# Twelve expert blocks of the first ten token tiles, worked from a table of their own while the last tiles are routed

## The chip, the cores and the metric

One core of one Trainium2 chip runs the whole program. Its engines are TensorE (PE), VectorE (DVE), ScalarE (ACT), GpSimd (POOL) and SyncE (SP), each with its own list of instructions that it works through in order; they wait for one another on semaphores. SP issues most of the DMA transfers, ACT some, POOL the indirect ones (gathers and scatters through a list of indices). The metric is the device time of one execution in microseconds; lower is better.

## The reference, cut to what matters

The program computes four layers on 2048 tokens (16 tiles of 128) of width 512. The change concerns the border between the first and the second:

```python
x = x + _L0_xattn_ref(_layernorm(x), ctx, seg, ...)      # attention, 16 heads
x = x + _L0_ffn_ref(_layernorm(x), gate_w, ...)          # mixture of experts
#   scores = softmax(h @ gate_w.T); topk_w, topk_idx = top_k(scores, 6)
#   for e in range(16):
#       y += cw[:, e] * ((silu(h @ w_gate[e].T) * (h @ w_up[e].T)) @ w_down[e].T)
x = x + _L1_xattn_ref(_layernorm(x), ctx, mask)
x = x + _L1_ffn_ref(_layernorm(x), ...)
```

Every token goes to 6 of 16 experts of inner width 352.

## The kernel before, in words

**Attention.** The loop runs over 64 steps `m` (`STEPS`): tile `m // 4`, four heads each. It is software pipelined: scores of step m, transposes of m-2, values of m-3, output products of m-4. Beside it run three side jobs: splitting the expert weights into two float16 halves in DRAM (`split_load`, `split_act`, `split_dve`, `split_store`, 128 pieces), writing the finished tiles' normalized rows to `token_rows` in DRAM (`row_stats`, `row_rstd`, `row_normalize`, `row_high`, `row_low`, `row_store`), and routing. Routing a tile is: transpose its rows (`token_rows` on PE), `logits`, softmax, the best six (`route_best`), a mask, `ranks` (a running count per expert by matmul), `route_rank`, and six indirect DMAs of POOL (`place`) that write each token's number to its place in the list of its expert (`recs`, `expert_tokens` in the trace). The last attention steps and the routing of tiles 14 and 15 stand behind the loop as code written out by hand.

**The table.** After tile 15, PE sums the counts of all experts (`count`), DVE makes a table of 111 blocks from it (L2007 to L2030), PE turns its columns into one row (`cols`), and DVE copies the row to `tabrow`. A block is up to 128 tokens of one expert; the row holds for each block the tile of `recs` where its list stands, the expert, and the slot of its weights.

**Experts.** SP waits for the table, for all stores and for all placements, then loads the lists (`records`, one DMA of 128 numbers a block), and the weights into a ring of 4 slots: `first_a` and `first_d` for the first four experts, `expert_loads` and `down_loads` for later ones (issued for each block and executed only at the last block of an expert). POOL gathers the token rows of a block (`gather_rows`, ring of 6). PE turns them (`turn_rows`), makes gate and up products (`expert_up`), turns the hidden values (`turn_hidden`) and makes the down product (`expert_down`); ACT scales it (`rows_out`, ring of 3), and POOL adds it to `x_sum` in DRAM by an indirect DMA that must have landed before the next is issued. The first blocks of every engine are a hand-written order of these calls.

What sets the order everywhere is the program text: no scheduler moves anything.

## Time and profile before

| | us |
|---|---|
| median of 3 runs | 1945.56 (1942.91 to 1946.44) |
| the profiled execution | 1929.01 |
| its span | 1927.2 |
| PE busy | 1803.6 (94%) |
| DVE busy | 1096.7 (57%) |
| ACT busy | 886.3 (46%) |
| POOL busy | 819.4 (43%) |

The profiled execution is 16.55 us shorter than the median of the runs. The span is what the trace covers; 1.8 us lie around it. A row of `windows` gives for a stretch of the span the busy time of each engine, the granted clock of PE as a share of full speed (1.00 is 2.4 GHz, 0.50 is 1.2 GHz), the share of time in which the DMA engines were busy, and what they moved. A row of a timeline gives the start, the duration, the engine, the line, the operation and, in brackets, how long the engine had been idle and what released it.

### The profile page before, as it was taken

How to read it: one execution, taken by the hardware profiler on the slowest of the kernel's cores; microseconds unless marked ns; L12 is line 12 of the kernel's file. 1: busy time of each engine (PE TensorE's matmuls, PEld its weight loads, DVE VectorE, ACT ScalarE, POOL GpSimd, SP SyncE). 2: the span in 40 equal slices, each digit the busy share in tenths (PEclk: the TensorE clock that was granted, in tenths of full speed). 3: DMA queues.
4: the chain of work that ended last, by engine and by line, in shares of the span. 5: the costliest groups of instructions: out<-in, count | busy, mean ns of one | idle time of the engine just before them, and what ended most of it. 6: DMA issues, size and time to landing. Idle time of an engine off the chain costs nothing.

```text
span 1927.2 us, 39654 instructions
## 1 busy us (share of the span) xinstructions
PE 1803.6 (94%) x12786; PEld 1075.3 (56%) x12789; DVE 1096.7 (57%) x2985; ACT 886.3 (46%) x1833; POOL 819.4 (43%) x731
## 2 busy tenths in 40 slices
PE   6989999999982999999999999995899999999998
PEld 3566667666641666666666666664644444444444
DVE  4678887888862333322323223223756877777776
ACT  4578878878851443434434434443832121122211
POOL 4224456666564334444443443442112434554442
PEclk8999999999986999999999999997999999999999
DMA  8255598878886566666666665545012355555653
GB/s 309 88 153 175 177 140 182 188 166 175 184 183 181 143 147 141 155 165 149 153 155 142 155 152 100 90 85 129 33 35 72 124 182 201 205 170 209 208 174 144
DMA packets 156354, 294.83 MB, mean 153 GB/s; under 512 B 41248, under 2 KB 91040, under 8 KB 152032
## 3 DMA queue, kind: packets, MB, share of 16 engines
q1 hardware_dynamic: 105184, 157.48, 30.4%
q0 software_dynamic: 46368, 126.29, 26.8%
q10 hardware_dynamic: 4608, 8.52, 1.6%
q8 instruction: 115, 1.88, 0.4%
q14 instruction: 79, 0.65, 0.1%
HBM read 426.00 MB, written 78.33 MB: 262 GB/s over the span
## 4 chain that ended last, share of the span: by engine, by line
PE 63%; DMA 15%; DVE 9%; issue 6%; ACT 5%; SPq 1%; POOL 1%; POOLq 0%; ACTq 0%; DVEq 0%
PE bank L235 16%; PE bank L236 16%; PE bank L237 16%; DMA x_sum<-x,work_arena 10%; DVE work_arena L1580 2%; PE bank L1064 2%; ACT xt_arena L1316 2%; DMA work_arena<-in_moe_w 2%; PE bank L854 1%; PE bank L1091 1%; DVE xt_arena L1580 1%; PE bank L1175 1%; DMA expert_w<-xt_arena 1%; DMA x<-token_rows,work_arena 1%; DVE xt_arena L1663 1%
## 5 line engine op out<-in xcount | busy, mean ns | idle before, releaser
L235 PE MATMUL bank<-work_arena,xt_arena 128*128 x1221 | 404.6, 331 | 2.8 <-DVE xt_arena L2074 1.9
L237 PE MATMUL bank<-work_arena,xt_arena 128*128 x1221 | 404.5, 331 | 0.0
L236 PE MATMUL bank<-work_arena,xt_arena 128*128 x1221 | 404.5, 331 | 0.0
L2313 POOL DMA_INDIRECT x_sum<-x,work_arena x111 | 175.9, 1585 | 397.7 <-DMA x_sum<-x,work_arena 197.2
L2062 DVE TENSOR_TENSOR xt_arena<-xt_arena,bank 128x352 f32<-128x352 f32 x111 | 57.9, 522 | 406.2 <-PE bank L237 406.2
L235 PE MATMUL bank<-work_arena 128*128 128x512 f16 (+1 forms) x600 | 226.8, 379 | 13.9 <-DVE x L1885 6.7
L236 PE MATMUL bank<-work_arena 128*128 128x512 f16 (+1 forms) x600 | 226.7, 379 | 0.0
L237 PE MATMUL bank<-work_arena 128*128 128x512 f16 (+1 forms) x600 | 226.6, 379 | 0.0
L1470 ACT ACTIVATE xt_arena<-bank 128x1024 f16<-128x1024 f16 x111 | 113.6, 1023 | 224.8 <-PE bank L1064 224.8
L235 PE MATMUL bank<-xt_arena,work_arena 128*128 128x512 f16 x528 | 200.4, 380 | 1.8 <-DVE xt_arena L195 1.8
L236 PE MATMUL bank<-xt_arena,work_arena 128*128 128x512 f16 x528 | 200.3, 379 | 0.0
L237 PE MATMUL bank<-xt_arena,work_arena 128*128 128x512 f16 x528 | 200.1, 379 | 0.0
L2320 POOL TENSOR_TENSOR work_arena<-work_arena 128x512 f16<-128x512 f32 x64 | 73.2, 1163 | 269.1 <-ACT work_arena L1455 269.1
L237 PEld LDWEIGHTS bank<-work_arena,xt_arena 128*128 128x128 f16 x1221 | 119.7, 98 | 85.0
L235 PEld LDWEIGHTS bank<-work_arena,xt_arena 128*128 128x128 f16 x1221 | 119.7, 98 | 82.6 <-issue 3.3
L236 PEld LDWEIGHTS bank<-work_arena,xt_arena 128*128 128x128 f16 x1221 | 119.7, 98 | 79.4
L2329 POOL DMA_INDIRECT work_arena<-in_pk_e,work_arena x128 | 135.0, 1055 | 36.8 <-issue 34.1
L1580 DVE SCALAR_TENSOR_TENSOR work_arena<-work_arena 128x704 f16<-128x704 f32 (+2 forms) x90 | 89.6, 997 | 73.3 <-ACT work_arena L1363 72.6
L2300 POOL DMA_INDIRECT x<-token_rows,work_arena x111 | 110.8, 999 | 46.3 <-issue 28.7
L2214 POOL TENSOR_TENSOR xt_arena<-xt_arena,work_arena 128x512 f32<-128x512 f32 x64 | 66.9, 1045 | 143.7 <-DVE work_arena L1670 137.7
L1316 ACT ACTIVATE xt_arena<-xt_arena,work_arena 128x128 f32<-128x128 f32 x256 | 123.2, 482 | 2.1
L1885 DVE SCALAR_TENSOR_TENSOR x<-bank,x 128x512 f32<-128x512 f32 x128 | 88.2, 691 | 60.4 <-PE bank L237 60.4
(278 smaller groups left out, 3817.5 us busy)
## 6 DMA issues: line engine op xcount, KB each, us to landing
work_arena<-expert_w SPq DMA_DIRECT2D x111, 1408.0 KB
work_arena<-expert_w SPq DMA_DIRECT2D x111, 768.0 KB
work_arena<-in_moe_w SPq DMA_DIRECT2D x64, 352.0 KB
expert_w<-work_arena SPq DMA_DIRECT2D x128, 176.0 KB
work_arena<-in_moe_w SPq DMA_DIRECT2D x64, 192.0 KB
expert_w<-xt_arena SPq DMA_DIRECT2D x128, 96.0 KB
work_arena<-in_mlp_w SPq DMA_DIRECT2D x8, 1536.0 KB, 9.0
work_arena<-in_head_w SPq DMA_DIRECT2D x16, 512.0 KB, 5.2
```

Source lines behind the costliest of these rows:

```text
L235: pe.matmul(o, a_hi, b_hi, start=start, stop=False)
L236: pe.matmul(o, a_hi, b_lo, start=False, stop=False)
L237: return pe.matmul(o, a_lo, b_hi, start=False, stop=stop)
L1316: last = act.activation(prob[:, m % 3, i, :], prob[:, m % 3, i, :], ACT.Exp, bias=ebias[:, m % 4, i:i + 1], scale=seg_scale[:, t:t + 1], a ...
L1470: act.activation(xT[:, b % 2, :], bank[4][:, :].bitcast(F16), ACT.Copy).then_inc(xt_cp, 1)
L1580: return dve.scalar_tensor_tensor(out=o, in0=src, scalar=scale, in1=hi, op0=ALU.mult, op1=ALU.subtract)
L1885: dve.scalar_tensor_tensor(out=xv, in0=bank[6 + q % 2][:, :], scalar=1 / (WS * WS), in1=xv, op0=ALU.mult, op1=ALU.add).then_inc(xadd[q % 2 ...
L2214: pool.tensor_tensor(prob[:, m % 3, :, :], prob[:, m % 3, :, :], rinv[:, m % 4, :].unsqueeze(2).to_broadcast([P, 4, P]), ALU.mult).then_in ...
L2300: pool.indirect_dma_start(out=xbu[:, b % XB, :], out_offset=None, in_=rows[:, :], in_offset=bass.IndirectOffsetOnAxis(ap=rid[:, i:i + 1], ...
L2313: pool.indirect_dma_start(out=xacc[:, :], out_offset=bass.IndirectOffsetOnAxis(ap=rid[:, i:i + 1], axis=0), in_=ysb[:, b % YB, :], in_offs ...
L2320: pool.tensor_tensor(h_lo[:, S_ % 2, c, :], m2[:, c, :], h_hi[:, S_ % 2, c, :], ALU.subtract).then_inc(hlo, 1)
L2329: pool.indirect_dma_start(out=gbuf[:, n % 2 * SETS + i - FIRST[n], :], out_offset=None, in_=ins["pk_e"][:, :], in_offset=bass.IndirectOffs ...
```

## The change

The list places of the first ten tiles are known well before the last tiles are routed. The new kernel counts the experts after tile 9 (`early_count`), makes a first table of the 12 first whole blocks in expert order (`early_blocks`, `early_columns`, `early_row`), and starts the expert stage with them. The tokens of tiles 0 to 9 give each expert 10 x 128 x 6 / 16 = 480 on average, which is three whole blocks, so that the twelve belong to about four experts; these are loaded again for the rest of their tokens. The last attention output, the rows of tile 15, its logits, mask, ranks and placements, the full count, the second table (`main_blocks`, `main_columns`, `main_row`) and its lists are moved in between the first expert blocks. The number of blocks is 111 as before. In outline (the diff, cut):

```diff
+EARLY_TILES, EARLY = 10, 12
+EARLY_Y = 9
@@ SP
             for e in range(E):
+                if e == E - 1:
+                    sp.wait_ge(yadd, 1)
+                    sp.dma_start(xacc[T:T + P, :], x[:, 0, :]).then_inc(xacc_early, 16)
+                    sp.wait_ge(rope_h, 2 * NT)
+                    sp.wait_ge(rope_l, 2 * NT)
+                    sp.dma_start(rc2, ins["route_c2"]).then_inc(route_in, 16)
                 for i in range(e * NPC, (e + 1) * NPC):
                     split_store(i)
...
-            sp.wait_ge(routed, TABLE_ROW)
+            sp.wait_ge(q_free, q_at["early_cols",] + 1)
...
+            sp.wait_ge(placed_early, 16 * TOPE * EARLY_TILES)
             records(0)
+            for s in range(STAGES):
+                sp.wait_ge(split_out[s], 32 * len(range(s, E * NPC, STAGES)))
+            sp.wait_ge(q_mm, q_at["heads", NT - 1, 3] + 1)
+            firsts = [first_expert(r) for r in range(SLOTS)]
+            first_a(0, firsts[0])
+            for r in range(SLOTS - 1):
+                first_d(r, firsts[r])
             records(1)
+            records(2)
+            sp.wait_ge(y_mm, STEPS)
+            first_a(1, firsts[1])
+            first_a(2, firsts[2])
+            first_d(3, firsts[3])
+            first_a(3, firsts[3])
             for b in range(NBLK + 5):
+                if b == EARLY_Y:
+                    sp.wait_ge(routed, TABLE_ROW)
...
+                    sp.wait_ge(placed, 16 * TOPE * (NT - EARLY_TILES))
+                    records(3)
+                    records(4)
@@ PE
-            pe.wait_ge(routed, TABLE_ROW)
+            pe.wait_ge(q_free, q_at["early_cols",] + 1)
             slots = {b: slot_of(b) for b in range(2)}
             turn_rows(0)
+            outputs(STEPS - 1)
+            expert_up(0, slots[0])
             turn_rows(1)
-            expert_up(0, slots[0])
             for b in range(NBLK - 3):
                 expert_up(b + 1, slots[b + 1])
+                if b == 0:
+                    token_rows(15)
+                if b == 1:
+                    logits(15)
+                if b + 2 == EARLY:
+                    pe.wait_ge(routed, TABLE_ROW)
                 slots[b + 2] = slot_of(b + 2)
                 turn_rows(b + 2)
                 turn_hidden(b)
                 if b > 0:
                     expert_down(b - 1, slots.pop(b - 1))
+                if b == 2:
+                    ranks(Q15)
+                if b == 3:
+                    route_count()
+                if b == 5:
+                    route_cols()
@@ DVE
+                if m == STEPS - 3:
+                    early_blocks()
+                if m == STEPS - 2:
+                    early_columns()
                 split_dve(m, 0)
...
             split_dve(STEPS - 1, 1)
+            early_row()
             add_outputs(14)
...
+                if b == 1:
+                    keep_logits(15)
+                    route_scores(Q15)
+                    route_softmax(Q15)
+                    route_best(Q15)
+                    route_mask(Q15)
+                if b == 2:
+                    route_rank(Q15)
+                if b == 3:
+                    main_blocks()
+                    main_columns()
+                if b == 5:
+                    main_row()
@@ POOL
+            normalize(STEPS - 1)
+            gather_rows(0)
+            gather_rows(1)
+            row_rstd(14)
+            row_low(14)
+            gather_rows(2)
+            gather_rows(3)
+            place_batch(INNER - 1, 0, TOPE)
+            gather_rows(4)
+            gather_rows(5)
+            place_batch(Q14, 0, 1)
+            row_rstd(15)
+            row_low(15)
+            place_batch(Q14, 1, TOPE)
+            gather_rows(6)
             for b in range(NBLK):
-                if b + ROWS_AHEAD < NBLK:
+                if b == 1:
+                    place_batch(Q15, 0, TOPE)
+                if ROWS_AHEAD + 2 <= b + ROWS_AHEAD < NBLK:
                     gather_rows(b + ROWS_AHEAD)
                 pool.wait_ge(y_cp, b + 1)
```

The first nine blocks put their down product into one PSUM bank (`y_bank`, bank 6) instead of two, since bank 7 holds the routing of tile 15 (logits, ranks, count, columns). On ACT, `row_high(15)`, `rows_turned(15)`, `gate_exps(Q15)` and `row_store(15)` move between the first blocks, and some small buffers move to other places in SBUF.

POOL, from the normalization of attention step 63 on. Lines of before: L2214 is that normalization, L2220 and L2224 are `row_rstd` and `row_low`, L2228 a placement, L2300 a gather, L2313 the addition to `x_sum`.

```order
L2214 TENSOR_TENSOR xt_arena<-xt_arena,work_arena 128x512 [waits recip]
L2220 TENSOR_TENSOR ln_rs<-ln_ve,neg_half 128x1 [waits t_stat]
L2224 TENSOR_TENSOR xt_arena<-xt_arena 128x512 [waits row_hi]
L2228 DMA expert_tokens<-work_arena 38784x1 [waits indexed]
L2228 DMA expert_tokens<-work_arena 38784x1 x5
L2228 DMA expert_tokens<-work_arena 38784x1 [waits indexed]
L2220 TENSOR_TENSOR ln_rs<-ln_ve,neg_half 128x1 [waits t_stat]
L2224 TENSOR_TENSOR xt_arena<-xt_arena 128x512 [waits row_hi]
```

Now, with the same operations at L2404, L2410, L2414, L2418, L2476 and L2504:

```order
L2404 TENSOR_TENSOR xt_arena<-xt_arena,work_arena 128x512 [waits recip]
L2476 DMA x<-token_rows,xt_arena 128x528 [waits rec_in0]
L2476 DMA x<-token_rows,xt_arena 128x528
L2410 TENSOR_TENSOR ln_rs<-ln_ve,neg_half 128x1 [waits t_stat]
L2414 TENSOR_TENSOR xt_arena<-xt_arena 128x512 [waits row_hi]
L2476 DMA x<-token_rows,xt_arena 128x528 x2
L2418 DMA expert_tokens<-work_arena 38784x1 [waits indexed]
L2418 DMA expert_tokens<-work_arena 38784x1 x5
L2476 DMA x<-token_rows,xt_arena 128x528 [waits rec_in1]
```

Two gathers, the first of which waits for the lists of blocks 0 to 3 (`rec_in0`), now stand ahead of the `row_rstd` and `row_low` of tile 14.

PE, behind the last but one attention output. Before, the last output (the second row), then tile 15 (L955, L235), its ranks (L973), the count (L1050), the table's columns (L1054), and only then the first rows of an expert block (L1064). In the fences that follow, the further rows of the same products are left out.

```order
L955 MATMUL bank<-id,xt_arena 128x128 [waits tr_cp,row_lo]
L955 MATMUL bank<-id,xt_arena 128x128 x7
L235 MATMUL bank<-xt_arena 128x16 [waits q_free,gate_s,tr_cp]
...
L973 MATMUL bank<-work_arena,xt_arena 128x16 [waits q_free,masked]
...
L1050 MATMUL bank<-work_arena,xt_arena 128x16 [waits q_free,masked]
L1054 MATMUL bank<-id,work_arena 1x128 [waits q_free,routed]
...
L1064 MATMUL bank<-id,x 128x128 [waits xb_in0]
```

Now the ranks of tile 14 (L1021), the rows of block 0 (L1125), the last attention output (the first L240), and the up products of block 0 (the L240 that waits for `load_a0`):

```order
L1021 MATMUL bank<-work_arena,xt_arena 128x16 [waits q_free,masked]
...
L1129 TENSOR_LOAD xt_arena [waits q_free]
...
L1125 MATMUL bank<-id,x 128x128 [waits smax,xb_in0]
L1125 MATMUL bank<-id,x 128x128 x7
L240 MATMUL bank<-work_arena 128x512 [waits otl]
...
L240 ISA [waits load_a0,e_xt_cp]
```

The chain over tile 15, count and columns is no longer ahead of the first block.

## Rows read from the trace of the kernel before

**Rows 1.** Windows: length; busy us of PE, PEld, DVE, ACT, POOL; clock, DMA share, GB/s.

```profile
620.00:625.00 5.00, 5.00 (x31) 3.13 (x30) 1.30 (x4) 1.18 (x3) 0.00 (x0) 0.89 1.02 422
667.00:717.00 50.00, 50.00 (x375) 31.79 (x374) 14.88 (x40) 20.14 (x32) 18.27 (x15) 1.00 0.69 167
```

**Rows 2.** Waits of PE between 550 and 660 us: total, times, longest.

```profile
PE bank L1064 <- DMA x<-token_rows,work_arena: 19.9, 1, 19.9
```

**Rows 3.** Chain that ended last, 525 to 620 us: start, us, what.

```profile
548.88 11.35 DMA work_arena<-in_moe_w
596.70 8.67 DMA expert_tokens<-work_arena
```

**Rows 4.** Timeline of PE.

```profile
568.17 0.62 PE L955 MATMUL bank<-id,xt_arena 128*128 128x128 f16 x8
577.75 0.38 PE L237 MATMUL bank<-work_arena 128*128 128x512 f16 x1
614.36 1.04 PE L1064 MATMUL bank<-id,x 128*128 128x128 f16 x8 [19.94 <-DMA x<-token_rows,work_arena]
617.40 0.50 PE L235 MATMUL bank<-work_arena,xt_arena 128*128 x1
621.14 0.31 PE L236 MATMUL bank<-work_arena,xt_arena 128*128 x1
```

**Rows 5.** Timeline of DVE.

```profile
550.42 0.89 DVE L1580 SCALAR_TENSOR_TENSOR work_arena<-work_arena 128x704 f16<-128x704 f32 x1 [2.68 <-ACT work_arena L1363]
560.81 0.56 DVE L1580 SCALAR_TENSOR_TENSOR xt_arena<-work_arena,xt_arena 128x384 f16<-128x384 f32 x1 [0.57 <-ACT xt_arena L1363]
589.82 0.41 DVE L2007 TENSOR_TENSOR work_arena<-bank,work_arena 128x240 f32<-128x240 f32 x1 [0.30 <-PE bank L1050]
591.25 0.17 DVE L2014 TENSOR_SCALAR work_arena<-work_arena 128x16 f32<-128x16 f32 x1
593.73 0.15 DVE L2030 SCALAR_TENSOR_TENSOR work_arena<-work_arena 128x1 f16<-128x1 f32 x1
```

**Rows 6.** Timeline of POOL.

```profile
562.14 1.03 POOL L2214 TENSOR_TENSOR xt_arena<-xt_arena,work_arena 128x512 f32<-128x512 f32 x1 [0.58 <-DVE work_arena L1670]
563.18 0.57 POOL L2220 TENSOR_TENSOR ln_rs<-ln_ve,neg_half 128x1 f32<-128x1 f32 x1
566.96 1.16 POOL L2224 TENSOR_TENSOR xt_arena<-xt_arena 128x512 f16<-128x512 f32 x1 [3.21 <-ACT xt_arena L1335]
594.14 0.97 POOL L2228 DMA_INDIRECT expert_tokens<-work_arena  x1 [0.30 <-issue]
609.26 2.64 POOL L2300 DMA_INDIRECT x<-token_rows,work_arena  x1 [11.60 <-DMA work_arena<-expert_tokens]
612.21 1.05 POOL L2300 DMA_INDIRECT x<-token_rows,work_arena  x1 [0.30 <-issue]
```

**Rows 7.** Timeline of SP's queue.

```profile
605.44 0.34 SPq L768 DMA_DIRECT2D work_arena<-expert_tokens  x1
606.84 7.38 SPq L717 DMA_DIRECT2D work_arena<-expert_tokens  x7
614.27 0.43 SPq L695 DMA_DIRECT2D work_arena<-expert_w  x1
```

**Rows 8.** Transfers to `x_sum`, 600 to 760 us: landing; two of them on POOL.

```profile
DMA to landing us min/median/max: 4.6/4.9/10.3
682.78 1.58 POOL L2313 DMA_INDIRECT x_sum<-x,work_arena  x1 [2.85 <-DMA x_sum<-x,work_arena]
688.31 1.58 POOL L2313 DMA_INDIRECT x_sum<-x,work_arena  x1 [2.65 <-DMA x_sum<-x,work_arena]
```

**Rows 9.** Gathers, 600 to 624 us: landing; then two turns of a block on PE.

```profile
DMA to landing us min/median/max: 7.3/7.6/7.9
675.89 0.61 PE L1064 MATMUL bank<-id,x 128*128 128x128 f16 x8
682.20 0.61 PE L1064 MATMUL bank<-id,x 128*128 128x128 f16 x8
```

More of the change, by code:

```diff
@@ L397, in build @@
         Q14, Q15 = INNER, INNER + 1
+        EARLY_Q = next(q for q, (a, _) in enumerate(BATCHES) if a == EARLY_TILES)
+        COUNT_AT = ready(EARLY_Q) + 2
         def batch_of(t):
@@ L1027, in _ @@
                     outputs(m - 4)
+                if m == COUNT_AT:
+                    pe.wait_ge(masked, EARLY_Q + 1)
+                    q_room_free(pe, "early_count")
+                    pe.matmul(q_bank("early_count")[:, 0:E], one16, seen16, start=True, stop=True).then_inc(q_mm, 1)
                 if m in RANK_AT:
                     ranks(RANK_AT[m])
+            pe.wait_ge(routed, EARLY_SET)
+            q_room_free(pe, "early_cols")
+            for i in range(4):
+                last = pe.matmul(q_bank("early_cols")[0:1, i * P:(i + 1) * P], tcol16[:, i:i + 1], id16[:, :],
+                                 start=True, stop=True)
+            last.then_inc(q_mm, 1)
             turn_prob(STEPS - 2)
@@ L2040, in memory_masks, with main_row @@
+            def main_row():
+                dve.wait_ge(q_mm, q_at["cols",] + 1)
+                n = NBLK - EARLY
+                for i in range(3):
+                    m = dve.tensor_copy(tabrow[0:1, i * P + EARLY:i * P + NBLK],
+                                        q_bank("cols")[0:1, i * P:i * P + n])
+                m.then_inc(routed, 1)
             def memory_masks(part):
@@ L2077, in _ @@
                 dve.memset(t[:, :, MOE_D:], 0.0)
+            add_outputs(15)
+            row_stats(15)
+            for s in range(STAGES):
+                dve.wait_ge(split_out[s], 32 * len(range(s, E * NPC, STAGES)))
+            choose(0, EARLY, early_end)
+            row_normalize(15)
+            expert_weight(0)
             hidden(0)
```

348 lines of the change are left out of this document (210 added, 138 removed).

## The prediction

> **What bounds the kernel now.** I read the windows over the span first, then the waits of PE around the border of attention and experts, then the chain that ended last, then the timelines of PE, DVE, POOL and SP there. Over the expert stage PE is the bound: 50.00 of 50 us busy between 667 and 717, DVE 14.88, ACT 20.14, POOL 18.27 [rows 1], one block each 6.31 us (675.89 to 682.20) [rows 9]. That stage holds the same 111 blocks afterwards and has nothing to give. What can be given is the border. The last attention output ends at 578.1, the first up product of an expert starts at 617.40: 39.3 us with only the short products of tile 15 in them [rows 4]. Its longest part is one wait of 19.94 us for the gathered rows [rows 2, 4]. The chain tells why: POOL's last placement starts at 596.70 and lands 8.67 us later [rows 3], SP fetches the first list at 605.44, POOL can gather at 609.26, PE has the rows at 614.36 [rows 4, 6, 7]. All of it hangs on tile 15, the last to be routed.
>
> **What goes.** The first blocks no longer wait for tile 15, its placements, the count and the table. If nothing else were late, the up product of block 0 would follow the last output at once: 617.40 - 578.1 = 39.3 us. So the question is what is late next. I follow three chains.
>
> **The early table on DVE.** `early_blocks` is 11 instructions, five of them 240 to 256 elements wide. The widest of before took 0.41 us, a small one 0.17, and the 18 instructions of the table of before needed 593.88 - 589.82 = 4.06 us with their waits on each other [rows 5]. 5 x 0.43 + 6 x 0.18 = 3.2 us, and `early_columns`, 30 small ones at 0.17, 5.1 us. They stand in attention steps 61 and 62. The first is ahead of a split of expert weights and of the maxima of step 62, so its 3.2 us pass to ScalarE's exponentials and the next split, and on; it also waits for a constant table (`route_c2`) whose load now stands among the split transfers, where one load took 11.35 us to land [rows 3]; for that I add 1 us (between 0 and 4). The second fits partly into the 2.68 us in which DVE waited for ScalarE at 550.42 [rows 5]. The last piece of the split ended at 561.37 [rows 5]; DVE's extra 9.3 us less the 2.7 us of idle time and less some of the load's 11.35 us, which was waiting in a queue that has drained by then, leave 5 us: 566.4 (bounds: 0, all hidden by that load, and 9). The copy `early_row` comes behind it.
>
> **The lists, and what stands behind POOL.** SP issues four lists, the first 606.84 - 605.44 = 1.4 us after its wait and 1.17 us apart (seven take 7.38 us) [rows 7]: the row is there at 566.8, the last list goes out at 571.7. A list took from 605.44 to 609.26 = 3.8 us in an empty queue [rows 6, 7]: 575.5. The stores of the last split pieces go ahead in the same queue, so not less. POOL finished the normalization of step 63 at 563.2 [rows 6], now some 5 us later, 568. It then stands at the first gather until 575.4, and two gathers take 2.64 + 0.3 + 1.05 = 4.0 us [rows 6]: 579.4. Behind them are queued `row_rstd(14)` and `row_low(14)`. This is the new wait, and everything is queued behind it: DVE's `row_normalize(14)`, ScalarE's `row_high(14)`, and on PE `token_rows(14)`, ahead of the last three outputs. From the start of `row_rstd` to that of the transposes on PE it took 568.17 - 563.18 = 5.0 us, of which 1.3 us were other work of DVE: 3.7 us [rows 4, 6]. PE gets there at 583.1 instead of 568.17.
>
> From there to the end of the last output PE needed 578.1 - 568.17 = 9.9 us [rows 4]. It will have been idle for 14 us. After the idle stretch of before the granted clock was at its low level for the first products: 13 of 128x352 started between 617.40 and 621.14, 0.29 us apart, where a block that has 24 such products, 9 of 512 columns and the turns takes 6.31 us later, 0.15 for each of the 24 [rows 4, 9]. I add 3 us. **Block 0 starts at 583.1 + 9.9 + 3 = 596.0**, 21.4 us earlier than before. Block 0 of before lost 13 x 0.14 = 1.8 us to the low clock; that is not repeated, since it is counted among the 3 us.
>
> **What is added or late among the first blocks.** (a) PE's work on tile 15, count and columns is done there at full clock: the transposes 0.45 and about 20 short products, 1.4 us. (b) `first_a(1)` is issued when the last output is done, 596; 1.4 MB at 422 GB/s [rows 1] are 3.4 us, and with the 3.8 us of a small transfer 7.2 us; block 1 wants it 4.1 us after block 0 began: 3 us (bounds 0 and 6). (c) POOL: `row_low(14)` to 583, gathers 2 and 3, six placements at 0.97 + 0.30 = 1.27 [rows 6] and gathers 4 and 5 to 596, one placement, then `row_rstd(15)` at 598 and the end of `row_low(15)` at 601.5. PE comes to `token_rows(15)` at 604 at the earliest, so nothing. (d) POOL then stands in front of its addition of block 1 until the ranks of tile 15 (PE, behind the down product of block 1, some 25 us after block 0 began: 621), and six placements hold it until 629.7. The gather of block 7 goes out behind that addition at 632. Gathers took 7.3 to 7.9 us from issue to landing [rows 9], but PE had its rows 614.36 - 609.26 = 5.1 us after POOL's start [rows 4, 6]; I take 6.5: 638.5. PE wants it before the down product of block 4: 621 + 3 x 6.31 - 2.3 = 637.6. 1 us (bounds 0 and 6). The additions to `x_sum` fall 9 us behind and follow each other at 688.31 - 682.78 = 5.5 us against 6.3 of PE [rows 8], so they catch up; the ring of three absorbs them. (e) The second table: count behind the down product of block 2, the row at 644, its need before block 12 at about 660; hidden with 16 us. (f) ScalarE loads its function table twice more around `gate_exps(15)`; it is busy 20 of 50 us [rows 1], nothing. (g) Four experts loaded twice: 4 x 2.2 MB = 8.7 MB more over the first 75 us, 115 GB/s on top of the 167 [rows 1], under the 422 reached: nothing, unless additions slow down (a rival below).
>
> **The sum.** 21.4 + 1.8 - 1.4 - 3 - 1 = 17.8 us less. The profiled execution would be 1929.0 - 17.8 = 1911.2. The runs' median lies 16.55 us above that execution; I take the difference from the median, **1945.56 - 17.8 = 1928 us**. The likeliest case's own range, from the bounds of the three waits, is 1921 to 1935.
>
> The Trainium skill (DMA: Bandwidth & Descriptors, on HWDGE ordering) says that the transfers of one issuing engine are taken in ring order on each DMA engine. This would put the lists of blocks 4 to 7 behind the 3.7 MB of the first weights, that is 8.8 us more; no row here shows a list behind a weight load. By it the lists would be there at about 587, still ahead of POOL's gather 4 at 593, which is why it does not change the sum; at the mean rate it is rival 2.
>
> **The rivals.**
> 1. The border closes better: the DVE work hides wholly behind the load of 11.35 us, and the lists come at 570, because the row is there at 561. Then POOL goes on at 574, the transposes of tile 14 start at 578, fewer outputs run at the low clock (1 us instead of 3), and block 0 starts at 589; with no wait for weights or for block 7 the gain is 28.4 + 1.8 - 1.4 = 29. For it: DVE's idle times of 2.68 us and more before each split [rows 5]. Against it: DVE is the releaser of the chain there. 1917 us.
> 2. POOL is later than PE. The first weights, 3.7 MB from about 575, at the mean of 167 GB/s [rows 1] take 22 us; if the lists of blocks 4 to 7 come behind them at 601, POOL stands 8 us at gather 4, and `row_rstd(15)`, `row_normalize(15)`, `hidden(0)` and `token_rows(15)` stand behind it. For it: the mean rate of a busy stretch. Against it: with 422 GB/s, which such loads reached [rows 1], they are there by 590. It costs 8 us more: 1936 us.
> 3. The other side: the reloaded experts slow the additions. Each must land before the next is issued; their period is landing plus 0.65 us (5.5 with the median of 4.9) [rows 8]. PE waits for them as soon as the landing is over 5.65 us on average. 18 blocks (twelve early and two short runs behind them) have an expert load every 19 us instead of 44. At a landing of 8 us they cost 18 x (8.65 - 6.3) - 5 of slack = 37 us, and the time is 1965. It decides from 6.9 us. For it: a maximum of 10.3 us [rows 8]. Against it: the median of 4.9 in a stretch that has expert loads in it, and PE without idle time there [rows 1].
> 4. The time stays, because the gap is moved only (2 and a mild 3 together): 1944.
>
> **Chances.** The forecast 0.53, rival 1 0.20, rival 2 0.15, rival 3 0.06, rival 4 0.06. A measurement of this kernel can tell 0.2% (3.9 us) from no change. Faster: 0.53 + 0.20 + 0.15 and a little of the rest, 0.88; same 0.05; slower 0.07. The range that takes in rival 1, and rival 2 for the most part, is 1914 to 1941.
>
> **What would show it.** Right: the first up product of block 0 between 591 and 601 us (span of the new profile); a wait of PE of over 10 us in front of the transposes of tile 14, with POOL's two gathers ahead of them; the clock at its low level in the outputs behind it; a wait of some 3 us for the weights in front of block 1; no wait for the second table; block period 6.3 us from block 8 on. Wrong: if PE runs through the outputs without that wait (then rival 1), if PE waits at `token_rows(15)` or for hidden values (rival 2), or if additions land in over 7 us on average up to block 18 (rival 3). If the attention stage before 540 us changed its length, the argument would miss a cost there.

## The result and the profile after

The kernel after takes **1960.83 us** (median of 7 runs, 1957.08 to 1965.88); the kernel before, in the same session, 1945.56 us (7 runs, 1940.36 to 1951.59). The ratio is 1.0075, 95% interval [1.0056, 1.0093]: 15 us slower, where 17.8 us faster was forecast, outside the range of 1914 to 1941. In a second session it was 1940.34 against 1925.76: ratio 1.0069 [1.0041, 1.0097], 14.6 us slower. A session ("call" in the expectations below) is a set of runs on one chip in which the kernel before runs beside the others.

The profiled execution of after took 1960.83 us (span 1959.0), as its median. That of before was 16.5 us faster than the median of its runs, so the two spans differ by twice what the kernels do. Sessions differ by more than the kernels (before took 1924 to 1946 us in six of them; the one chip known to have come twice gave 1923.89 and 1927.74), so below ratios within one session are compared, and two traces are laid on each other at the start of `row_rstd(13)` on POOL, ahead of everything that the change moves at the border: 549.54 us in after, 535.17 in before. Another profile of each kernel has it at 530.85 (after, execution of 1939.67) and 532.64 (before, 1929.50); these two are close and are used for the account.

Timeline of ScalarE in that second profile of before (start us, us, engine, line, operation, then idle time and releaser): the copies of the rows of blocks 12, 20 and 110.

```profile
688.61 1.02 ACT L1470 ACTIVATE xt_arena<-bank 128x1024 f16<-128x1024 f16 x1 [1.77 <-PE bank L1064]
739.04 1.02 ACT L1470 ACTIVATE xt_arena<-bank 128x1024 f16<-128x1024 f16 x1 [1.77 <-PE bank L1064]
1311.94 1.02 ACT L1470 ACTIVATE xt_arena<-bank 128x1024 f16<-128x1024 f16 x1 [1.77 <-PE bank L1064]
```

The same three copies in the second profile of after.

```profile
690.66 1.02 ACT L1543 ACTIVATE xt_arena<-bank 128x1024 f16<-128x1024 f16 x1 [4.07 <-PE bank L1125]
752.07 1.02 ACT L1543 ACTIVATE xt_arena<-bank 128x1024 f16<-128x1024 f16 x1 [1.77 <-PE bank L1125]
1321.39 1.02 ACT L1543 ACTIVATE xt_arena<-bank 128x1024 f16<-128x1024 f16 x1 [1.77 <-PE bank L1125]
```

Block 0's first up product starts at 617.33 in before and at 588.97 in after: **28.4 us earlier**, 26.6 without the 1.8 us by which this execution of after was ahead already. At block 12 after is 2.1 us late, at block 20 it is 13.0 us late, at block 110 9.5. So the gain at the border is there in full, the early blocks lose 30.4 us and the eight behind them 11.0 more. Where PE stood in that time is in its timeline. The same profile of after, 575 to 725 us, answering to [rows 4] and [rows 2]:

```profile
575.38 1.03 PE L1003 MATMUL bank<-id,xt_arena 128*128 128x128 f16 x8 [7.96 <-POOL xt_arena L2414]
588.97 0.31 PE L240 MATMUL bank<-work_arena,xt_arena 128*128 x1
605.83 0.47 PE L240 MATMUL bank<-work_arena,xt_arena 128*128 x1 [12.67 <-ACT xt_arena L1543]
653.97 1.04 PE L1125 MATMUL bank<-id,x 128*128 128x128 f16 x8 [9.24 <-DMA x<-token_rows,xt_arena]
690.01 0.62 PE L1125 MATMUL bank<-id,x 128*128 128x128 f16 x8 [2.13 <-DMA x<-token_rows,xt_arena]
700.27 0.62 PE L1125 MATMUL bank<-id,x 128*128 128x128 f16 x8 [3.79 <-DMA x<-token_rows,xt_arena]
723.39 1.03 PE L1125 MATMUL bank<-id,x 128*128 128x128 f16 x8 [4.03 <-DMA x<-token_rows,xt_arena]
```

The wait of 19.94 us in front of the first turn is gone. In its place are 12.67 us in front of block 1 and 9.24 us in front of the turn of block 7, then three more for gathered rows: 31.9 us in five waits. Two short waits, for a copy (1.33 us) and for weights (1.16 us), add 2.5. The other 7 us of the 41 were not split; tile 15's products and low clock after the long pauses (0.68 granted from 653 to 660) are in them.

What stands behind the 12.67 us is in POOL's timeline of the same profile [rows 6]. Gather 4 waits for the lists of blocks 4 to 7, `row_rstd(15)` (L2410) stands behind it, and on it hang `row_normalize(15)`, `row_high(15)` and, behind that in ScalarE's order, the copy of block 1's rows:

```profile
569.98 1.00 POOL L2476 DMA_INDIRECT x<-token_rows,xt_arena  x1 [7.08 <-DMA xt_arena<-expert_tokens]
572.27 0.58 POOL L2410 TENSOR_TENSOR ln_rs<-ln_ve,neg_half 128x1 f32<-128x1 f32 x1
597.50 0.99 POOL L2476 DMA_INDIRECT x<-token_rows,xt_arena  x1 [11.97 <-DMA xt_arena<-expert_tokens]
601.09 0.62 POOL L2410 TENSOR_TENSOR ln_rs<-ln_ve,neg_half 128x1 f32<-128x1 f32 x1
```

And in the first profile of after, SP's queue [rows 7]: the four first lists, the first weights, and behind them the lists that POOL waited 12.42 us for.

```profile
583.62 3.70 SPq L747 DMA_DIRECT2D xt_arena<-expert_tokens  x4
590.20 0.36 SPq L730 DMA_DIRECT2D work_arena<-expert_w  x1
590.75 1.82 SPq L735 DMA_DIRECT2D work_arena<-expert_w  x3
593.35 10.44 SPq L747 DMA_DIRECT2D xt_arena<-expert_tokens  x8
```

Windows of the first profile of after, as [rows 1] has them: PE 42.81 of 50 us where it was busy throughout, and DMA at 210 GB/s instead of 167. Additions to `x_sum` issued from 640 to 720 us land in 6.0 us (median), at most 11.0 [rows 8: 4.9 and 10.3].

```profile
667.00:717.00 50.00, 42.81 (x301) 25.88 (x300) 18.34 (x57) 16.77 (x27) 16.99 (x13) 0.97 0.77 210
```

In that first profile there is one thing more, a pause of 10.52 us of VectorE in front of `keep_logits(14)` and one of 9.59 us of ScalarE in front of `values_high(63)`, both over at 606.4, though PE had done both products by 600.4. There block 0 starts at 616.15 us, 66.6 us after `row_rstd(13)`, against 58.1 in the second profile.

```profile
606.45 0.18 DVE L1783 COPY work_arena<-bank 128x16 f32<-128x16 f32 x1 [10.52 <-remote]
606.43 0.60 ACT L1407 ACTIVATE work_arena<-bank 128x512 f16<-128x512 f32 x1 [9.59 <-remote]
```

### The profile page after: what moved, and what is told of

Same layout as the page of the kernel before. It is cut to its first block, busy times and chain, and to the rows that moved or that the text cites. A ratio compares the mean times of both kernels' runs of the same rounds, so it can differ in the third digit from the quotient of the medians.

```text
span 1959.0 us, 39977 instructions
## 1 busy us (share of the span) xinstructions
PE 1822.4 (93%) x12791; PEld 1079.0 (55%) x12794; DVE 1100.8 (56%) x3040; ACT 886.3 (45%) x1835; POOL 817.1 (42%) x731
## 2 busy tenths in 40 slices
DMA packets 157509, 303.77 MB, mean 155 GB/s; under 512 B 41376, under 2 KB 91168, under 8 KB 152672
## 4 chain that ended last, share of the span: by engine, by line
PE 69%; DMA 13%; DVE 7%; issue 5%; ACT 3%; SPq 1%; another core or an unknown queue 1%; POOL 1%; POOLq 1%; ACTq 0%; DVEq 0%
PE bank L240 18%; PE bank L241 18%; PE bank L242 18%; DMA x_sum<-x,xt_arena 8%; PE bank L1125 2%; DVE work_arena L1663 2%; PE bank L902 1%; PE bank L1154 1%; DMA work_arena<-expert_w 1%; DMA work_arena<-in_moe_w 1%; PE bank L978 1%; DMA x<-token_rows,xt_arena 1%; ACT xt_arena L1394 1%; PE bank L893 1%
## 5 line engine op out<-in xcount | busy, mean ns | idle before, releaser
L240 PE MATMUL bank<-work_arena,xt_arena 128*128 x1221 | 406.3, 333 | 11.0 <-ACT xt_arena L1543 8.0
L2504 POOL DMA_INDIRECT x_sum<-x,xt_arena x111 | 176.1, 1586 | 403.2 <-DMA x_sum<-x,xt_arena 217.9
L240 PE MATMUL bank<-work_arena 128*128 128x512 f16 (+1 forms) x600 | 230.4, 385 | 16.6 <-DVE x L2034 6.8
L241 PE MATMUL bank<-work_arena 128*128 128x512 f16 (+1 forms) x600 | 229.9, 385 | 0.0
L242 PE MATMUL bank<-work_arena 128*128 128x512 f16 (+1 forms) x600 | 229.4, 384 | 0.0
L240 PE MATMUL bank<-xt_arena,work_arena 128*128 128x512 f16 x528 | 200.4, 380 | 1.8 <-DVE xt_arena L200 1.8
L240 PEld LDWEIGHTS bank<-work_arena,xt_arena 128*128 128x128 f16 x1221 | 120.1, 98 | 92.4 <-issue 13.3
L2476 POOL DMA_INDIRECT x<-token_rows,xt_arena x111 | 111.4, 1004 | 51.4 <-issue 27.3
L2404 POOL TENSOR_TENSOR xt_arena<-xt_arena,work_arena 128x512 f32<-128x512 f32 x64 | 66.7, 1042 | 142.1 <-DVE work_arena L1752 134.3
L1563 ACT ACTIVATE x<-bank,work_arena 128x512 f32<-128x512 f32 x111 | 76.2, 687 | 105.3 <-PE bank L242 96.0
```

Of the source, the lines that this page charges most:

```text
L240: pe.matmul(o, a_hi, b_hi, start=start, stop=False)
L241: pe.matmul(o, a_hi, b_lo, start=False, stop=False)
L242: return pe.matmul(o, a_lo, b_hi, start=False, stop=stop)
L1563: act.activation(ysb[:, b % YB, :], y_bank(b)[:, :], ACT.Copy, scale=ecw[:, b % 4, :]).then_inc(y_cp, 1)
L2404: pool.tensor_tensor(prob[:, m % 3, :, :], prob[:, m % 3, :, :], rinv[:, m % 4, :].unsqueeze(2).to_broadcast([P, 4, P]), ALU.mult).then_in ...
L2476: pool.indirect_dma_start(out=xbu[:, b % XB, :], out_offset=None, in_=rows[:, :], in_offset=bass.IndirectOffsetOnAxis(ap=rid[:, i:i + 1], ...
```

## The experiments

Five theories were tried. A: the wait for lists behind the first weights (SP) and POOL's order. B: the four reloaded experts (8.9 MB: the page of after has 303.77 MB, of before 294.83). C: the batch of tile 15's placements in POOL's queue. D: transfers of one queue share the engines, so that the weights of block 1 come late. E: placements in flight slow every other transfer. "Placement" is one of POOL's indirect DMAs that write 128 list entries of 4 bytes. The kernels called "left out" give the tokens of tiles 13 to 15 no expert; all others compute everything. The time of before in each session stands in its first row:

| run | median us | before us | ratio, 95% interval |
|---|---|---|---|
| session 1: lists first | 1952.25 | 1923.89 | 1.0150 [1.0133, 1.0167] |
| row 14 first | 1948.22 | | 1.0138 [1.0121, 1.0155] |
| no reload | 1935.49 | | 1.0051 [1.0031, 1.0071] |
| session 2: after again | 1940.34 | 1925.76 | 1.0069 [1.0041, 1.0097] |
| placements of tile 15 spread | 1937.05 | | 1.0059 [1.0038, 1.0080] |
| four edits | 1939.70 | | 1.0070 [1.0048, 1.0091] |
| four edits, reload skipped | 1929.60 | | 1.0014 [0.9992, 1.0037] |
| session 3: weights order | 1944.21 | 1945.95 | 0.9999 [0.9969, 1.0029] |
| placed later | 1940.24 | | 0.9963 [0.9930, 0.9996] |
| ScalarE's order | 1941.44 | | 0.9982 [0.9953, 1.0011] |
| the same, reload kept | 1958.66 | | 1.0061 [1.0033, 1.0089] |
| session 4: late placements left out | 1905.76 | 1927.74 | 0.9890 [0.9855, 0.9925] |
| four edits, reload skipped, again | 1926.55 | | 0.9996 [0.9976, 1.0016] |
| early weights | 1920.22 | | 0.9965 [0.9935, 0.9995] |
| early weights, placements spread | 1924.70 | | 0.9985 [0.9959, 1.0012] |
| session 5: lists, then early weights | 1940.89 | 1945.14 | 0.9981 [0.9957, 1.0005] |
| after, late placements left out | 1933.79 | | 0.9933 [0.9908, 0.9958] |

**Before once more**, unchanged.

> The kernel before, unchanged, profiled once more. If the first profiled execution of it was untypically fast (1929.0 against a median of 1945.6), this one is near 1945 and POOL starts row_rstd(13) at 546 to 550 instead of 535.2: then most of the 14.4 us by which the kernel after reached attention step 61 later is no cost of the change. If the change itself made the attention stage longer, this profile has row_rstd(13) at 535 to 538 again.

1929.50 us, `row_rstd(13)` at 532.64. Both branches missed something: before's median was 1923.89 in session 1, so 1929.5 is not an unusually short execution here. With after's second profile at 530.85 the change does not lengthen the attention stage in the sessions in which before takes 1924 to 1928 us, where all profiles have `row_rstd(13)` at 527.8 to 536.8. In the sessions in which before takes 1945 us the changed kernels have it at 545.9 to 553.5, and before was profiled there only in an execution 16.5 us under its median (535.17). That the 14.4 us of the first pair lie between executions is likely by this, and was not shown in such a session.

**Lists first.**

```
+            records(1)        # behind records(0), ahead of the first weights
-            records(1)        # behind the first weights
```

> The kernel after, with the lists of blocks 4 to 7 issued ahead of the 3.7 MB of first weights in SP's queue. Theory A (the wait of 12.4 us of POOL in front of gather 4 holds row_rstd(15), row_high(15) and with them rows_copy(1), and so blocks 1 and 2): POOL's wait falls under 3 us, the up product of block 1 starts 5 to 8 us earlier, the kernel is 5 to 10 us faster than after, 1951 to 1956 us. Theory B (the first twelve blocks are slow because the reloaded experts take DMA time): the lists come early but the block period stays, 1959 to 1961.

The lists come early and POOL's wait at gather 4 is gone (584.13 us, 0.30 idle). PE's wait is not; another stands in the same place, for the up weights of block 1, issued at 589.8:

```profile
607.91 0.47 PE L240 MATMUL bank<-work_arena,xt_arena 128*128 x1 [14.28 <-DMA work_arena<-expert_w]
```

So A is true of the wait and false of the time: nothing is gained. By the ratios the kernel is even slower than after (1.0150 against 1.0075 and 1.0069), but after did not run beside it, and the profile is of the shortest execution (1939.03 us, the other four 1950 to 1955), so what cost the difference was not found. Block 1 has two late inputs, and the change had hidden the second behind the first.

**Row 14 first.**

```
+            row_rstd(14)
+            row_low(14)
             gather_rows(0)
             gather_rows(1)
-            row_rstd(14)
-            row_low(14)
```

> The kernel after, with POOL's row_rstd(14) and row_low(14) ahead of the gathers of blocks 0 and 1, so that tile 14 does not wait for the lists. By the prediction's step (the wait for the lists is the new bound): PE's wait of 5.7 us at the transposes of tile 14 goes, and block 0 starts 5 to 9 us earlier; 1952 to 1956 us. Rival: the pause of 10.5 us of VectorE and ScalarE that ended together at 606.4 ends with the burst of first weights, whatever came before it; then PE gains the 5.7 us and gives them back at the ranks of tile 14, and the time stays at 1959 to 1961.

`row_rstd(14)` starts at 563.87 instead of some 570, and PE does not wait in front of tile 14, but no time is gained (1.0138, again above after's ratios, and again with a profile of the shortest execution, 1936.10 us, the other four 1948 to 1951). What the prediction called the new bound was not one: block 0 is some 6 us earlier, and PE then waits 21.36 us in front of block 1.

**No reload.**

```
-                last, ahead = (64, 0) if b < EARLY else (E - SLOTS, SLOTS)
+                last, ahead = (0, 0) if b < EARLY else (E - SLOTS, SLOTS)
```

> The kernel after without the loads at the end of each early run (with this data the early runs and the first runs of the long table are experts 0 to 3 in the same slots, so nothing is computed differently): 8.7 MB less. Rival 3 of the prediction and theory B (reloads slow the blocks): the first twelve blocks take 6.3 us each again and the gather waits up to block 53 go; 20 to 30 us faster, 1931 to 1940. Theory A (waits of POOL and of tile 15's work): 0 to 4 us faster, 1957 to 1961.

13 to 17 us faster than the two kernels beside it, but each of these has another edit, and against after's ratios of the other sessions it is 0.2% only. The clean pairs on B come below. From block 0's copy to block 12's it still takes 95.6 us (73.7 and 73.2 in before's profiles, 104.1 in after's second). B is a part and not the whole.

**After again.**

> The kernel after, unchanged, for a second profile and as the measure of the runs beside it. If the pause of 10.5 us of VectorE and ScalarE before 606 belongs to the order of the work it is there again; if it was a disturbance of that one execution, PE waits under 1 us at the ranks of tile 14 and block 0's rows are copied 59 to 60 us after row_rstd(13), as without the reload. The ratio to before is 1.006 to 1.015.

The ratio is as expected. The pause of 10.5 us is not there (PE waits 0.43 us at the ranks); this is the second profile above.

**Placements of tile 15 spread.**

```
-                if b == 1:
-                    place_batch(Q15, 0, TOPE)
+                if b in (2, 3, 4):          # behind the gather of block b + 5
+                    place_batch(Q15, 2 * b - 4, 2 * b - 2)
```

> The kernel after, with the six placements of tile 15 not in one batch ahead of the addition of block 1, but two each behind the gathers of blocks 7, 8 and 9. Theory C (POOL's queue: the batch waits for the ranks of tile 15 and holds additions and gathers for 14 us, and from then on PE follows POOL): the wait of 4 to 8 us of PE in front of the turn of block 7 goes, 5 to 10 us faster than the kernel after. Theory B (the reloads alone, through the landing of the additions): additions land as late as before, at most 2 us faster.

The wait of 9.2 us in front of block 7 goes; one of 4.3 us comes later, and weights are late twice (1.7 and 3.8 us). 3 us of medians, intervals overlap: C is the cause of the wait, but worth little alone.

**Four edits, and four edits with the reload skipped.** Lists first, row 14 first, the placements spread, and a wait of SP for the weights of block 1 before the next are issued; in the second kernel also

```
+                then(dve.tensor_tensor(tcol[:, 8:9], tcol[:, 11:12], tcol[:, 0:1], ALU.is_equal))
+                then(dve.tensor_tensor(tcol[:, 4:5], tcol[:, 4:5], tcol[:, 8:9], ALU.max))
```

> Four edits on the kernel after, the reloads kept: lists of blocks 4 to 7 ahead of the first weights; row_rstd(14) and row_low(14) ahead of the first gathers; placements of tile 15 spread; the weights of the third and fourth run issued only when block 1's have landed. Theory A + C (queues of SP and POOL): each gives 3 to 10 us, together 15 to 25 us faster than after, about equal to before or up to 8 us faster. Theory B (reloads): at most 8 us faster than after, and additions still land in 8 us and more around the reloads. Weights of block 1, 17.9 us from issue to landing when four loads were issued together, land in 6 to 9 us.

> As the one with four edits, and an early run whose next expert is the one that its slot holds already does not load it again (two more instructions of VectorE in early_columns; here all four). Theory B: 12 to 17 us faster than with the reloads, as the kernel without reloads was against the two beside it. Theory A + C: the queues were the cause, so 0 to 5 us faster. Faster than before by 10 to 20 us if both hold.

Four repairs of queues together gave 0.6 us: A and C fall as an account of the loss by themselves. PE waits 7.5 and 3.6 us for the weights of block 0 in them, and 15.5 and 20.1 us for those of block 1. Skipping four reloads gave 10.1 us (B).

**Weights in order, placements later, ScalarE's order, reload kept.** On the kernel with the reload skipped, each on top of the one before: SP issues up weights of run 1, lists, down weights of run 1, and at the last output the up weights of run 2 alone; POOL takes `pool.wait_ge(load_a[1], 16)` ahead of the placements of tiles 13 and 14 (the expectation's "12 to 14" is wrong); ScalarE copies the rows of block 1 ahead of `row_high(15)`. The fourth is the third with the reloads.

> The kernel with four edits and no reload of an expert that is there, and now the first weights in the order in which they are needed, a run at a time: up weights of run 1 behind the first lists, down weights of run 1, then at the last output the up weights of run 2 alone, and the rest only when these have landed. Theory D (transfers of one queue share the engines, so that the first issued lands last; block 1 waited 20.1 us for its weights because 3.7 MB went beside them): the wait falls to 3 to 8 us, and with it the kernel to 10 to 15 us under the one without this order, 1.4% above before there: ratio 0.993 to 0.996. Theory E (the engines are slow between 588 and 616 us, 100 to 250 GB/s at a busy share near 1, because 12 placements of 4-byte records are in flight): 1.4 MB still take 12 us and more, at most 6 us gained.

> As the one before it in this call, and POOL issues the twelve placements of tiles 12 to 14 only when the up weights of run 2 have landed (row_rstd(15) and the gathers of blocks 4 to 6 go ahead of them). Theory E: these weights land in 5 to 7 us, DMA moves 350 GB/s and more in that stretch, 5 to 10 us faster than the kernel beside it. Theory D alone: no change within 3 us.

> As the one with later placements, and ScalarE copies the rows of block 1 ahead of row_high(15). If ScalarE's order is the wait behind the weights (12.7 us in the second profile of after, hidden behind the weights in the others), PE waits under 2 us in front of block 1's up product and the kernel is 1 to 5 us faster than the one beside it; if the weights are still last there, no change. Against before: 10 to 20 us faster if D and E hold.

> As the one with ScalarE's order, but each early run loads its next expert again, as the kernel after does. Theory B (8.7 MB within some 70 us beside the additions and gathers): 8 to 15 us slower than the kernel beside it that skips them. If the reloads cost only because the first weights were late: under 4 us.

The order gained nothing clear (0.9999 against 1.0014, two sessions), so D's 10 to 15 us did not come: PE waits 11.09 us for block 1's weights, and 4.32 at block 2. With the placements later the wait at block 1 is 4.86 us, as E has it, and the kernel 4 us faster, within the intervals and short of the 5 to 10 that E expected; 11.89 us stand at block 2 instead, where ScalarE and VectorE pause beside the delayed placements as in the first profile of after. ScalarE's order gave nothing. The reloads cost 17.2 us here (1958.66 against 1941.44), the second pair on B.

**The late placements left out, and kept.** Removed are the 18 placements of tiles 13, 14 and 15; gathers, products and additions stay as many, with pad rows in the lists.

```
-            place_batch(INNER - 1, 0, TOPE)
-            place_batch(Q14, 0, 1)
-            place_batch(Q14, 1, TOPE)
-                if b in (2, 3, 4):
-                    place_batch(Q15, 2 * b - 4, 2 * b - 2)
```

> The kernel with four edits and no reload of an expert that is there, but the 18 placements of tiles 13, 14 and 15 are left out (their tokens get no expert, and the slots of the lists stay pads; gathers, products and additions are as many). Theory E (4-byte placements in flight make every weight packet slow): the weights of block 1 land in 8 to 10 us instead of 20 to 28, DMA moves over 300 GB/s between block 0 and block 1, packets take 0.4 us each instead of 1.6, and the kernel is 10 to 15 us faster than the one with them in this call. Theory D (shared queue, 3.7 MB beside them): under 4 us faster.

> The same with the placements, as it ran before, for the comparison on one chip: ratio to before 0.999 to 1.004, PE waits 15 us and more for the weights of block 1.

20.8 us faster than its twin in the same session. Queues in the stretch 580 to 588 us, without the placements (packets, MB, share of 16 engines; q1 is SP's queue, here the weights in packets of 6 and 11 KB, q0 POOL's, q10 ScalarE's):

```profile
q1 hardware_dynamic: 315, 1.94, 59.0%
q0 software_dynamic: 239, 0.81, 26.0%
q10 hardware_dynamic: 240, 0.47, 15.0%
```

The same stretch of the twin, with 6 placements issued just before it (573.0 to 579.5 us) and 2 in it:

```profile
q1 hardware_dynamic: 195, 1.09, 83.2%
q10 hardware_dynamic: 185, 0.35, 14.2%
q0 software_dynamic: 123, 0.01, 2.3%
```

The engines are busy all the time in both (share 1.00), but move 402 GB/s in the one and 182 in the other. Worked out for q1: 1.94 MB in 59.0% of 16 x 8 us are 25.7 GB/s per engine, 1.09 MB in 83.2% are 10.2. The placements' own packets fill 2.3%, and the others are slow beside them. PE's wait for block 1's weights fell from 17.27 to 9.11 us.

The lists could be a rival, since they too move in packets of 4 bytes. They are not the cause: in the last kernel below, from 604 to 608 us, over 1100 packets of q1 pass, most of them lists, and no placement, and q10 keeps 24 GB/s per engine. In after's second profile q10 has 24 to 25 GB/s per engine from 580 to 586 us and 3.6 to 6.2 from 586 to 592. In between q0 changes from the packets of gathers (0.24 MB in 2 us) to packets that move next to nothing, those of the placements issued from 578.05 on.

**Early weights.** On four edits with the reload skipped: the up weights of run 2 go out when `outputs(61)` is done (their slot overlaps only output weights of heads 0 to 5), and ScalarE's order. SP's list changes in more than that: the lists of blocks 4 to 7 stand behind these two loads, the down weights of runs 2 and 3 behind the up weights of run 3, and the wait for block 1's weights is gone. The part about the early load:

```
             first_a(0, firsts[0])
+            sp.wait_ge(y_mm, STEPS - 2)
+            first_a(1, firsts[1])
             records(1)
             first_d(0, firsts[0])
             sp.wait_ge(y_mm, STEPS)
-            first_a(1, firsts[1])
```

> Lists of blocks 0 to 3, then the up weights of run 1, and those of run 2 as soon as outputs(61) is done (their slot overlaps only output weights of heads 0 to 5), two steps before the last output; down weights behind them, ScalarE copies the rows of block 1 ahead of row_high(15), no reload of what is there. If the late issue was the cause, PE waits under 6 us in front of block 1 and the kernel is 8 to 15 us faster than the one with four edits: ratio to before 0.991 to 0.996. If the placements in flight slow whatever is loaded then (theory E), the wait moves to block 2 or 3 and at most 5 us are gained.

> As the one before, and the 18 placements of tiles 13 to 15 come only when the first four runs' up weights have landed, from then on three or six a block. Theory E: waits for weights in blocks 1 to 3 under 8 us in all, ratio to before 0.988 to 0.994. Theory D alone: no better than the one before.

> As the one with early weights, and the lists of blocks 4 to 7 go ahead of the second run's up weights: gather 4 of POOL starts before 590 us, row_rstd(15) at 589 to 592 instead of 602, no wait of PE at the transposes of tile 15 (2.8 us there). If POOL's wait for these lists still counts, 3 to 6 us faster than the one with early weights, ratio to before 0.992 to 0.995; if placements in flight decide when the weights land (theory E), the wait for the weights of block 1 grows by what the lists gain: 0.995 to 0.999.

The first has 0.9965 [0.9935, 0.9995]: 6.3 us under its neighbour, with overlapping intervals, and 0.35% under before. With the placements later (0.9963) it is the fastest of the kernels that compute everything. The waits for weights are 3.5, 4.5 and 2.2 us. With the placements held back until the weights of four runs are there, the weights fly (592 to 604 us: 4.93 MB, 411 GB/s), block 4's rows are copied at 613.2 instead of 623.0, and then gathers are late (1.9, 4.1 and 5.2 us of PE) beside the spread placements: it ends 4.5 us slower, within the intervals, where E expected 0.988 to 0.994 (0.9985 measured). E is right about the weights and was wrong about the gain: moved, the placements cost elsewhere. Lists ahead of the early weights gave nothing (0.9981, as E's branch expected).

**After itself without the late placements.** No other edit.

> The kernel after without any edit, but the 18 placements of tiles 13, 14 and 15 are left out (their tokens get no expert). Theory E: after's 14 us over before are mostly theirs, this kernel is 12 to 20 us faster than after, ratio to before 0.997 to 1.001. If POOL's wait for the lists of blocks 4 to 7 behind the first weights decides in the kernel after (rival 2), it stays at 12 us and the gain is under 6 us, ratio 1.004 to 1.008.

1933.79 us, ratio 0.9933 [0.9908, 0.9958]. Against after's 1.0075 and 1.0069 that is 1.4%, some 27 us, more than expected. From the copy of block 0's rows to that of block 12's it takes 79.2 us there (104.1 in after's second profile, 73.7 in before), PE waits 3.00 us in front of block 1 and not at all in front of block 7:

```profile
616.12 0.47 PE L240 MATMUL bank<-work_arena,xt_arena 128*128 x1 [3.00 <-ACT xt_arena L1543]
716.03 1.03 PE L1125 MATMUL bank<-id,x 128*128 128x128 f16 x8 [5.44 <-DMA x<-token_rows,xt_arena]
```

POOL still stands at gather 4 for the lists behind the first weights, as the branch for rival 2 expected:

```profile
609.17 0.95 POOL L2476 DMA_INDIRECT x<-token_rows,xt_arena  x1 [11.16 <-DMA xt_arena<-expert_tokens]
```

POOL comes there 7.8 us after its first gather instead of 15.6, for it has no six placements to issue before, and gather 4 goes out 15.0 us after the first of these lists was issued, against 22.5 in after's second profile. So a wait of 11 us of POOL remains and most of PE's wait does not. Leaving the placements out also spares POOL 18 x 1.28 = 23 us and lets pads be gathered, so the 27 us are not the slowed packets alone. The share of each was not separated.

## Why the prediction was wrong

**The border: right.** Block 0 was put at 596.0 us, 60.8 us after `row_rstd(13)`; it came 58.1 us after it in the second profile (66.6 in the first, with the unexplained pause). POOL stood 7.08 us at the first gather, with `row_rstd(14)` behind it (predicted 7.4), and the clock was at its low level in the transposes and outputs behind it (0.50 granted from 575 to 579). One sign was missed: PE waited 7.96 us in front of tile 14 where the working has 14 and the sign asked for over 10; the transposes came 44.5 us after `row_rstd(13)`, put at 47.9. The gain is 26.6 us against 21.4.

**(c), "so nothing": wrong by 12.7 us.** The prediction had the lists of blocks 4 to 7 at 587 even by the ring rule, ahead of POOL's gather 4. POOL got to gather 4 at 585.5 and the lists at 597.5. The late lists are rival 2, put at 8 us and 0.15, and it was the case. More than PE's transposes of tile 15 hung on them: ScalarE's `row_high(15)` stands ahead of the copy of block 1's rows, which the working did not follow. With the lists issued first POOL did not wait (0.30 us); with the placements left out it still waited 11.16 us. So the order in SP's queue makes the wait, and the placements lengthen what the lists take (22.5 us with them, 15.0 without).

**(b), 3 us for block 1's weights, bounds 0 and 6: wrong by more than twice the upper bound.** It is hidden behind (c) in after; where the lists go first it is 14.3 to 20.1 us, and 9.1 us without the late placements. Its price came from 1.4 MB at the 422 GB/s of [rows 1]. That row is from a stretch without placements (the last one is issued at 596.70 and lands 8.67 us later [rows 3]). The stretch that was asked for has them, and before's trace shows it. Its window answering to [rows 1], where placements and the first weights overlap under a PE that has next to nothing to do:

```profile
584.00:600.00 16.00, 1.48 (x20) 0.85 (x19) 7.11 (x37) 1.24 (x2) 10.12 (x11) 0.50 0.98 198
```

The engines are busy 0.98 of it at 198 GB/s. In before PE did not wait for weights there, since the slow stretch lay in the 39 us gap. The change closes the gap and puts the slow stretch on PE's path.

**(d), 1 us in front of block 7: measured 9.24.** The chain was the predicted one (ranks, six placements, addition, gather; the gather went out at 639.86, put at 632), but it landed 14.1 us later, not 6.5. Spreading the six placements took this wait away and gave little time.

**(g), "nothing" for 8.7 MB: measured 10.1 and 17.2 us** in two pairs of repaired kernels that differ in that alone. The reason given, 167 + 115 under 422 GB/s, again counts bytes. Rival 3 had the sign and put its threshold at a mean landing of 6.9 us; the median was 6.3 in the second profile (600 to 720 us, at most 15.2) and 6.0 in the first. PE waited for gathers in the same POOL queue and not for additions, so the threshold was of the wrong quantity.

**The sum.** The forecast was -21.4 - 1.8 + 1.4 + 3 + 1. Measured in the pair of profiles: -1.8 ahead of the border, -26.6 there, +30.4 over the early blocks, +11.0 over the next eight, -3.6 behind: +9.5 at block 110, 10.3 of span. The medians differ by 14.6; the other 4 us are between executions and not placed. The terms of the border were right to a few us. The terms behind it, 4 us in the sum, were each priced by a rate or a landing from a stretch without placements, and without the 18 late ones the change does make the program faster: by 0.67%, or 11 us, in a kernel that leaves their tokens out. The chance of 0.88 for faster took (b), (c), (d) and (g) as if they were independent, though all four are transfers priced in the same way.

Open are three things: which part of the 27 us is slowed packets and which POOL's time; why large packets are slow beside placements; and the pauses of VectorE and ScalarE. Pauses of 3 to 12 us with no releaser in the record are in the profiles of the changed kernels from the three sessions where before took 1945 us (between 565 and 640 us, beside placements and weight loads), with one exception: the kernel without the late placements. The profile of before from such a session has none either, nor has any from the sessions with 1924 to 1928 us. Whether they are a cost of the placements too was not tried by itself.

## What to carry to other kernels

Closing a gap removes what it hid: before crediting the gap, list the transfers that ran in it and price them at the rate of that stretch (bytes over busy share), not at the best rate of the page. Many small scattered writes can cost their neighbours more than themselves, so look whether a load that something waits for flies beside them; here loading early gained 6 us, and moving the writes only moved the waits. When a wait has two late inputs, removing one shows nothing: look in the trace for the one that takes its place before the theory is dropped.

## What the hardware showed

- SP's weight packets (6 and 11 KB) moved at 25.7 GB/s per engine without placements in flight and at 10.2 beside them, the engines at a busy share of 1.00 both times. POOL's queue, with the placements of 128 records of 4 bytes, took 2.3% of the engines itself.
- The Trainium skill (DMA: Bandwidth & Descriptors, the table at its head) puts the line rate at transfers of 512 B and more, with a read-modify-write below. The trace agrees as to the rate: the 123 packets of POOL's queue in the twin's stretch moved 0.01 MB in 2.3% of 16 x 8 us, an estimate of 3 GB/s per engine. That large transfers beside them lose 60% of their rate is what these runs add.
- Up weights issued first at 580.94 us, ahead of three down loads of the same queue, were there only at 593.67 (kernel with four edits): 12.7 us, in which all 3.7 MB fit at 290 GB/s. Placements were in flight there too. Without them the same load took from 575.89 to 583.51 us, 7.6 us, where its own 1.4 MB at the 402 GB/s of that kernel are 3.5 us: part of the delay is there without placements.
- Two executions of after differ by 18.7 us in the attention stage alone (`row_rstd(13)` at 549.54 and 530.85 us, in two sessions); over all profiles it starts at 527.8 to 553.5 us.
